# Products of constants on TensorE during eight waits of a two-layer perceiver kernel

## The reference

```python
x = x + L0_xattn(_layernorm(x), ctx)   # 16 heads of 16, queries from x, keys and values from ctx, then a 2-layer MLP
x = x + L0_attn(_layernorm(x))         # causal self-attention over the 128 tokens, 16 heads
x = x + L0_ffn(_layernorm(x))          # 8 experts, gelu, weighted by the 2 largest gate probabilities
x = x + L1_xattn(_layernorm(x), ctx)   # 16 heads of 64
x = x + L1_attn(_layernorm(x), W)      # softmax(x x^T / 16), split at 0.01: kept part times x, small part times W
x = x + L1_ffn(_layernorm(x))          # 8 gated experts (silu), weighted by 2
```

## Time and profile before

| | |
|---|---|
| runs, median (lowest to highest) | 1458.98 us (1455.98 to 1460.86), 3 runs |
| profiled execution, own time | 1454.85 us |
| its span, first to last instruction | 1453.1 us |
| TensorE matmul busy | 1346.4 us, 93% |
| TensorE weight load busy | 886.7 us, 61% |
| VectorE busy | 1072.4 us, 74% |
| ScalarE busy | 1120.5 us, 77% |
| GpSimd busy | 198.7 us, 14% |
| mean granted TensorE clock | 0.978 of full speed |

### The profile page before, as it was taken

One profiled execution on the slowest core, in us unless ns is written; L12 is line 12 of the kernel. 1 busy time (PEld: TensorE's weight loads), 2 busy tenths in 40 slices (PEclk: granted clock), 3 DMA queues, 4 the chain that ended last, 5 costly groups with the idle time before them and its releaser, 6 DMA issues.

```text
span 1453.1 us, 37662 instructions
## 1 busy us (share of the span) xinstructions
PE 1346.4 (93%) x15514; PEld 886.7 (61%) x15514; DVE 1072.4 (74%) x1556; ACT 1120.5 (77%) x1646; POOL 198.7 (14%) x195
## 2 busy tenths in 40 slices
PE   5888887899999898999999979999999999999979
PEld 2444444677776694333333357777776777777758
DVE  6999999100000776999999988888888888888864
ACT  3787876798987465888888868888887888888831
POOL 6322211000000006000000000000000004440720
PEclk7999999999999999999999999999999999999989
DMA  4355435775755564556655566777777589988810
GB/s 143 135 191 185 159 137 153 195 183 141 189 139 157 182 238 141 190 191 222 216 191 190 191 133 134 144 153 154 147 145 144 115 172 195 189 177 174 230 45 5
DMA packets 128848, 236.54 MB, mean 163 GB/s; under 512 B 9292, under 2 KB 114214, under 8 KB 128678
## 3 DMA queue, kind: packets, MB, share of 16 engines
q1 hardware_dynamic: 128678, 234.13, 60.7%
HBM read 155.98 MB, written 78.12 MB: 161 GB/s over the span
## 4 chain that ended last, share of the span: by engine, by line
PE 78%; DVE 13%; issue 5%; ACT 3%; DMA 1%; SPq 0%; POOL 0%; POOLq 0%; DVEq 0%; ACTq 0%
PE ps L794 78%; DVE small L1559 4%; DVE W L1493 3%; DMA W<-in_ctx_dram 1%; ACT W L1297 1%; DVE W L1523 1%; DVE p L1493 1%; DVE q_all L1493 1%; ACT p L1312 0%; DVE ctxT_b L1545 0%; ACT ps L1274 0%; DVE att L1493 0%; DVE ctxT_a_lo L1549 0%; ACT p L1274 0%; DVE stage L1493 0%
## 5 line engine op out<-in xcount | busy, mean ns | idle before, releaser
L1493 DVE TENSOR_TENSOR p<-ps,p 128x512 f16<-128x512 f32 (+1 forms) x467 | 350.9, 752 | 62.8 <-ACT ps L1274 60.4
L1274 ACT ACTIVATE p<-ps 128x512 f16<-128x512 f32 (+1 forms) x490 | 329.2, 682 | 78.8 <-PE ps L794 76.4
L794 PEld LDWEIGHTS ps<-q_all,W 128*128 128x128 f16 (+1 forms) x3544 | 229.3, 99 | 68.5 <-issue 11.8
L794 PE MATMUL ps<-q_all,W 128*128 128x128 f16 (+2 forms) x3544 | 262.9, 226 | 6.4 <-DVE p L1493 4.4
L1274 ACT ACTIVATE ps<-ps 128x512 f32<-128x512 f32 x392 | 235.8, 601 | 0.0
L794 PE MATMUL ps<-v,p 128*128 128x130 f16 x3136 | 168.7, 206 | 7.1 <-DVE p L1493 2.7
L794 PE MATMUL ps<-wv,ctxT_a_hi 128*128 128x512 f16 (+1 forms) x588 | 155.6, 346 | 10.1 <-DVE W L1523 5.9
L794 PEld LDWEIGHTS ps<-v,p 128*128 128x128 f16 x3136 | 146.7, 97 | 13.9 <-issue 4.5
L1660 DVE COPY att<-ps 128x512 f32<-128x512 f32 x1 | 0.7, 692 | 203.3 <-PE ps L794 203.3
L1493 DVE TENSOR_TENSOR v<-ps,v 128x512 f16<-128x512 f32 x196 | 135.6, 692 | 17.0 <-ACT v L1370 4.5
L794 PE MATMUL ps<-wv,ctxT_b 128*128 128x512 f16 (+1 forms) x504 | 137.0, 340 | 0.0
(11 more groups left out here) (274 smaller groups left out, 1997.0 us busy)
## 6 DMA issues: line engine op xcount, KB each, us to landing
W<-keys_hi SPq DMA_DIRECT2D x54, 896.0 KB, 8.1
W<-keys_low SPq DMA_DIRECT2D x27, 896.0 KB, 11.9
keys_hi<-p SPq DMA_DIRECT2D x75, 224.0 KB, 1.9
keys_low<-p SPq DMA_DIRECT2D x75, 224.0 KB, 1.9
keys_hi<-W SPq DMA_DIRECT2D x65, 224.0 KB, 1.9
keys_low<-W SPq DMA_DIRECT2D x65, 224.0 KB, 1.9
W<-values SPq DMA_DIRECT2D x14, 960.0 KB, 9.1
W<-in_L_ffn_W_dram SPq DMA_DIRECT2D x10, 1024.0 KB, 10.0
```

The costliest lines, as they stand in the source:

```text
L794: return pe.matmul(out_, lhsT, rhs, start=start, stop=stop, **kw)
L1274: return act.activation(out_, in_, ACT.Exp, scale=scale)
L1493: return dve.tensor_tensor(out_, a, b, op)
```

## The change

A helper `run_on(bank, n)` issues `n` products of `ident16` with 512 columns of itself into a PSUM bank. Nobody reads the results, and no semaphore is raised. It is called at eight points in TensorE's program, always ahead of a wait, with 79 products in all. No other engine's program changes.

```diff
+            def run_on(bank, n):
+
+                for _ in range(n):
+                    mm(ps[:, bank, :], ident16[:, :], bc(ident16[:, :], 1, [P, 4, P]), True, True)
+
...
                 if L is L0:
+                    run_on(T0_BANK, 20)
                     pe.wait_ge(shift_made, 1)
                     pe.wait_ge(values0_out, 4 * NCH)
...
                             if t == 0:
+                                if j == 0:
+                                    run_on(T0_BANK, 5)
                                 pe.wait_ge(rows_made, j + 1)
...
             pe.wait_ge(step_act, A_VTOK)
+            run_on(0, 8)
 
             def quarter(r):
...
+            run_on(2, 14)
             turn_xn(2, 0)
...
+            run_on(0, 9)
             turn_xn(3, 6)
             project_q(L1)
...
+            run_on(2, 7)
             turn_xn(4, 0)
             pe.wait_ge(ln_made, 5)
             for a in range(2):
                 ins = mm(ps[:, 1, 0:P], xnT[:, a, :], xnT[:, a, :], a == 0, a == 1)
             ins.then_inc(step_pe, 1)
+            run_on(2, 7)
             pe.wait_ge(step_dve, D_MASK)
...
+            run_on(1, 9)
             turn_xn(5, 0)
```

## The result

The changed kernel takes 1447.64 us (median of 4 runs, 1444.54 to 1450.91) against 1459.78 us. The ratio is 0.9925, with a 95% interval of 0.9904 to 0.9945. Measured once more beside 21 runs of the kernel before, it is 1446.91 against 1458.57 us, 0.9922 (0.9903 to 0.9941). So it gains 11.7 us by the medians, and 11.4 us by the ratio, with an interval of 8.6 to 14.1. The forecast was 7.5, with bounds of 4.4 and 9.1.

What follows compares the result with a forecast made beforehand. TensorE, 78% of the chain, bounds the kernel, and its clock falls at five places the change touches. The terms 0.6 + 0.1 + 1.0 + 2.7 + 3.1 = 7.5 us came off 1458.98: 1451.5 us, range 1446 to 1457.

Steps and rivals of the forecast that it cites:

- The price of the products: At all eight calls: 79 products take 17.1 us inside 21.9 us of idle time, so their own cost is nothing.
- The thinnest cover: Ahead of the first scores: the products end 0.44 us before the idle time does, the smallest such margin.
- The slower rival: At the lower clock the 79 products take 34 us and overrun their waits, 12 us more: 1471 us; chance 0.05.
- products of constants don't hold it: Products of constants don't hold the clock, or a wait behind each stage takes the gain: 1459 us; chance 0.10.
- The partial rival: Clock still falls at the second self-attention, 4.4 us remain, or also the first expert, 3.4 remain: 1454.6 to 1455.6; chance 0.15.
- the tail: Second self-attention and first gated expert, 1404.0 to 1415.3 us: full clock there gives 3.1 us (2.0 to 3.6).
- the experts: First expert, 497.3 to 500.6 us: its 32 pieces at full clock give 1.0 us (0.8 to 1.46).
- start of layer 1: 552.1 to 558.6 us: the projection's 32 pieces and two transposes at full clock give 2.7 us (1.2 to 2.7).
- self-attention: First self-attention, 483.1 to 487.0 us: the part ends on VectorE, so 0.1 us (0 to 0.9).
- I take the same gain off the median: Whole kernel: the 7.5 us found in one profiled execution are taken off the runs' median, 1458.98 us, giving 1451.5.
- The start of attention 0: Layer 0's attention start: transpose and first scores at full clock bring the first exponential forward, 0.6 us (0.4 to 0.7).

Runs made afterwards that it cites:

- only_attention0_start: Changed kernel with only the 20 and 5 products at the start of layer 0's attention, other calls at 0; 1456.21 us, ratio 0.9986 to the kernel before.
- the tiny kernel: Changed kernel with each of the 79 products cut to one column of weights and one of data; 1459.77 us, ratio 1.0005 to the kernel before.
- the experts' part alone: Changed kernel with only the 8 products in the self-attention and the 14 ahead of the third norm's transposes; 1458.74 us, ratio 0.9999 to the kernel before.
- more places: Changed kernel with six more calls, 35 more products; 1444.45 us, ratio 0.9903 to the kernel before.
- half: Changed kernel with 37 products in place of 79 at the same eight calls; 1448.90 us, ratio 0.9945 to the kernel before.
- double: Changed kernel with 158 products in place of 79 at the same eight calls; 1454.21 us.
- all_but_attention0_start: Changed kernel without the 20 and 5 products at the start of layer 0's attention; 1452.78 us, ratio 0.9962 to the kernel before.
- tiny_at_attention0_start: Changed kernel with the 25 products at the start of layer 0's attention cut to one column, the other 54 full; 1451.04 us, ratio 0.9947 to the kernel before.

## Why the prediction was right, and where a size was off

The forecast was faster, and by the mechanism that it named. Its steps:

- The price of the products: nothing. Right in both profiles of the changed kernel: 0.22 us each, ended 0.36 to 0.75 us early at seven places. The thinnest cover, forecast as 0.44 us, was 0.15. The cover is not safe, though. The slower rival's overrun cost 7.3 us for 12 forecast when it was built, and it also came unbuilt, for 0.9 us in only_attention0_start, where the clock fell ahead of the place. The rival's "against it", that such a call begins right behind a run of products, did not help there: the fall came within that run.
- What holds the clock. The tiny kernel shows it to be the work in the products. The rival "products of constants don't hold it" falls with 12.9 us. The partial rival holds in one of its two places, and in some executions, though not at the likelier: the tail never fell with its full products (-3.57 or -3.56 in every profile), but the experts did in the second profile of the changed kernel, in the experts' part alone and with more places. There the stretch is only -0.01 and not -1.30, with 0.75 or 0.76 us of idle time ahead of the transposes in all six. The Trainium skill's rule (TensorE: Matmul & The Clock Gate, A second HAM failure mode: psum-queue depth-cycling) stands in between: short idles of 0.15 to 0.75 us did no harm at four places and sometimes did at the fifth.
- The sizes. The sum took the gain from one profile, place by place. Against that profile the terms were near: experts 1.30 for 1.0, start of layer 1 2.62 for 2.7, tail 3.57 for 3.1, self-attention 0.21 for 0.1. The upper ends of the prediction's terms add up to 9.36 and not to 9.1, which is below the measured 11.7 all the same. The step that was mis-sized is "I take the same gain off the median": a place without its products costs more in other runs. In the table, the mean over the profiles without the products of a place, less the mean over those with them in full (half and double left out, and the tiny kernel counted as without), is 0.9 us for the MLP and the self-attention (0.72 and -0.22); 1.7 at the experts (1.05 and -0.66); 2.15 at layer 1's start (-0.48 and -2.63); 4.0 at the tail (0.47 and -3.57); and 2.4 in the attention of layer 0 (1.00 and -1.38), where 0.6 was forecast. Their sum is 11.2 us, against 11.7 measured. It is near in part by luck. Of the 0.9, all but 0.15 comes from three profiles in which the clock fell at the start of the MLP, 1.55 us each, ahead of the 8 products, so a fair sum is 10.4. And the attention of layer 0 is a stretch of 234 us with pauses and falls of its own.
- The start of attention 0 is the term furthest off. 0.6 us (0.4 to 0.7) was for the first exponential alone. VectorE's last step of the shifts starts at 255.99 us in the kernel before and at 256.23 in the kernel after, and the first exponential at 259.42 and 258.84. So the distance went from 3.43 to 2.61 us, 0.8 us less. The term had nothing for the rest of the stretch, because ScalarE was busy 12.93 of 13.30 us right behind the start. But behind that there were pauses of TensorE for which ScalarE waited: 9.1 and 9.3 us from 262 to 455 us in the two profiles before, 7.9 and 8.1 after (the second without its first wait, which belongs to the start). With the same list, the stretch differs by 2.7 to 3.0 us with and without work in the 25 products. all_but_attention0_start and tiny_at_attention0_start put the place at some 4 to 6 us, and only_attention0_start at 2.0 (-0.7 to 5.0), with the overrun in its profile. How the clock at the start shortens what comes long behind it, no run here tells.

What stays open is why the parts measured alone give so little, although their mean clocks add up. The pauses in layer 1's attention are likely a part of it. Single profiles differ by 3 us in a stretch whose program is the same, and a finer answer would need many profiles of each kernel.

## What to carry to other kernels

Where TensorE waits ahead of a dense stage, here 2.1 to 5.0 us, look at the granted clock behind the wait. If it falls, products that fill the wait at full clock and end half a microsecond before its releaser were nearly free here, and half of them already kept 8 to 10 of 11.7 us. Put them ahead of the wait that ends last (more_places did not, at one place), and leave cover for a clock that falls before they begin (only_attention0_start had too little). Price such an edit from several profiles of the kernel before, not from one, because the place where the clock falls differs from run to run. And do not add up parts that were measured alone: here they gave 0.6 us by the ratios, and the whole 11.4.

One long wait was left unfilled in every kernel here. In the middle of layer 1's attention TensorE waits 2.6 us for VectorE, and the clock fell beside it in 12 of the 14 profiles. A row of the timeline and one of the windows, from the kernel before:

```profile
1123.21 0.62 PE L794 MATMUL ps<-q_all,W 128*128 128x128 f16 x8 [2.62 <-DVE p L1493]
...
1125.30:1128.60 3.30, 3.30 (x27) 2.40 (x26) 1.77 (x3) 0.87 (x2) 0.00 (x0) 0.54 1.09 209
```

What products would win there is not shown.

## What the hardware showed beside that

Adding instructions to TensorE's list moves pauses of TensorE far behind them, which the profile shows as "issue" (time in which it waited for nothing that the profile shows). With one-column products, whose own work is next to nothing, two pauses of the kernel before were gone and another came. TensorE's timeline of the kernel before, and then of the one with one-column products:

```profile
994.05 0.43 PE L794 MATMUL ps<-v,p 128*128 128x130 f16 x6 [1.25 <-issue]
...
1342.84 0.36 PE L794 MATMUL ps<-v,p 128*128 128x66 f16 x5 [1.03 <-issue]
```

```profile
1210.33 0.64 PE L794 MATMUL ps<-v,p 128*128 128x66 f16 x11 [1.39 <-issue]
```

That list was no slower or faster in sum (1.0005). But the lists with 22 and 31 more products ahead of that stretch showed 6.1 and 6.6 us of such pauses where the kernel before had 3.5.

The traces say more about where they stand. Number TensorE's records in order of time, with matmuls, weight loads and those of its sequencer. Behind 262 us, the 14 profiles have 91 such pauses of over 0.5 us, and all 91 end at a number that leaves 193 or 194 when divided by 256. Each also ends 1.2 to 1.8 us after a packet of the DMA queue "instruction" has landed. The page counts these packets, 124 of 16 KB each:

```profile
q8 instruction: 124, 2.03, 0.7%
```

So these pauses lie 256 records or a multiple of it apart, and added instructions move them to other work. 16 KB are 64 bytes for each of 256 instructions. The reading that TensorE waits there for its next block of instructions fits all 91. No run changed the loading alone, and why some borders have a pause and most have none is open. The pauses may bear on the clock too: behind 4 of the 19 that were longer than 1.6 us it fell within 1.6 us, as at 1241.8 us in the kernel after.
